# The normalisation of the expert results moved in among the expert tiles, with its transfers issued by ScalarE

## The reference

```python
x = x + _layernorm(_L0_attn_ref(_layernorm(x), wq, wk, wv, wo))
x = x + _layernorm(_L0_ffn_ref(_layernorm(x), g1, g2, w_down, ..., w1, w2, w3))
# the end of _L0_ffn_ref, with res the residual stream after its attention:
probs = jax.nn.softmax(t @ router_w, axis=-1)          # t: (4096, 128), 8 experts
vals, idx = jax.lax.top_k(probs, 2)
gate = ...                                             # two weights a token, sum 1
hid = silu(einsum('td,edf->tef', t, w1)) * einsum('td,edf->tef', t, w3)   # f: 256
y = einsum('ted,te->td', einsum('tef,efd->ted', hid, w2), gate)
return res + y
```

## Time and profile before

| | |
|---|---|
| runs | 777.09, 778.49, 778.08 us; median 778.08 |
| profiled execution | 779.29 us, its span 777.3 us |
| busy: TensorE, VectorE, ScalarE, GpSimd | 85%, 65%, 51%, 46% of the span |
| granted clock of TensorE, mean of the span | 0.950 of full |

### The profile page before, as it was taken

How to read it: one execution, slowest core, us unless ns; L and a number is a source line. 1 busy time by engine, 2 the same in 40 slices (tenths; PEclk the granted TensorE clock), 3 DMA queues, 4 the chain that set the end, 5 groups by cost and what they waited for, 6 DMA issues and landing times.

```text
span 777.3 us, 15273 instructions
## 1 busy us (share of the span) xinstructions
PE 660.4 (85%) x4861; PEld 394.9 (51%) x4914; DVE 503.1 (65%) x1623; ACT 396.0 (51%) x792; POOL 355.9 (46%) x398
## 2 busy tenths in 40 slices
PE   7976899999899799899989988979879799999900
PEld 3434456466466456546646644545534366666600
DVE  7465866968968677786876876766715144444456
ACT  3243376566476467456646635544521265655515
POOL 4150290391582566349147351640134155555565
PEclk9999799999999999999989999999989999999955
DMA  6101001001001000000100100100025332322163
GB/s 179 43 0 28 1 1 29 1 1 31 27 1 28 29 2 21 29 8 1 35 22 1 28 30 2 29 28 2 1 87 142 71 82 77 82 76 72 51 240 94
DMA packets 38008, 33.27 MB, mean 43 GB/s; under 512 B 6384, under 2 KB 33072, under 8 KB 37920
## 3 DMA queue, kind: packets, MB, share of 16 engines
q1 hardware_dynamic: 33616, 23.39, 11.3%
q0 software_dynamic: 4320, 8.92, 3.5%
HBM read 17.09 MB, written 12.01 MB: 37 GB/s over the span
## 4 chain that ended last, share of the span: by engine, by line
PE 51%; DVE 19%; POOL 14%; issue 9%; ACT 3%; SPq 2%; DMA 2%; another core or an unknown queue 1%; DVEq 0%; POOLq 0%; ACTq 0%
PE wide L979 8%; PE small L803 6%; PE small L758 5%; DVE nmax L1268 5%; PE wide L778 5%; PE small L995 4%; PE small L790 3%; PE small L820 3%; PE small L762 2%; PE small L849 2%; PE wide L733 2%; PE wide L783 2%; PE small L986 2%; POOL k_rows L1181 2%; DVE a_st L1249 2%
## 5 line engine op out<-in xcount | busy, mean ns | idle before, releaser
L1268 DVE TENSOR_REDUCE nmax<-small 128x1 f32<-128x512 f32 (+3 forms) x352 | 217.0, 637 | 66.2 <-PE small L762 46.9
L1077 ACT ACTIVATE pT<-wide 128x1024 f32<-128x1024 f32 x160 | 159.2, 1021 | 72.0 <-PE wide L783 57.5
L758 PE MATMUL small<-kz,qT 128*128 128x256 bf16 (+3 forms) x503 | 123.1, 306 | 22.1 <-DVE nmax L1268 15.4
L1197 POOL DMA_INDIRECT token_rows<-m_row,place_u x64 | 63.0, 984 | 122.3 <-DVE place_u L1473 85.7
L778 PE MATMUL wide<-qT,kz 128*128 128x384 bf16 (+3 forms) x492 | 95.4, 306 | 9.4 <-DVE qT L1414 7.6
L1215 POOL DMA_INDIRECT result_rows<-pT,dest x71 | 68.0, 957 | 67.8 <-issue 38.4
L803 PE MATMUL small<-pT,v_pad 128*5 128x512 f32 (+3 forms) x1024 | 82.0, 461 | 5.3 <-issue 5.3
L762 PE MATMUL small<-future_sb,idb 128*128 128x128 bf16 (+2 forms) x328 | 78.1, 238 | 0.6
L979 PE MATMUL wide<-kz,pT 128*128 x142 | 74.7, 608 | 1.4 <-ACT pT L1110 1.3
L758 PEld LDWEIGHTS small<-kz,qT 128*128 128x128 bf16 x512 | 43.9, 99 | 56.1 <-DVE nmax L1268 30.0
L1528 DVE TENSOR_TENSOR pT<-pT,wide 128x256 f32<-128x256 f32 x71 | 29.9, 421 | 61.2 <-ACT pT L1116 55.3
(11 more groups left out here) (200 smaller groups left out, 1248.4 us busy)
## 6 DMA issues: line engine op xcount, KB each, us to landing
pT<-token_rows SPq DMA_DIRECT2D x71, 65.0 KB
kz<-k_all SPq DMA_DIRECT2D x32, 128.0 KB, 2.4
kz<-result_rows SPq DMA_DIRECT2D x16, 256.0 KB, 5.5
x<-L_attn_x SPq DMA_DIRECT2D x8, 256.0 KB, 3.6
kz<-L_ffn_w SPq DMA_DIRECT2D x2, 1024.0 KB, 6.9
out<-x SPq DMA_DIRECT2D x8, 256.0 KB, 2.2
result_rows<-pT,dest POOLq DMA_INDIRECT x71
token_rows<-m_row,place_u POOLq DMA_INDIRECT x64
```

Source lines behind the costliest of these rows:

```text
L758: pe.matmul(bank[:, at:at + keys], qT1[:, m.parity, g, tile * P:(tile + 1) * P], kz[:, m.parity, g, r, 0:keys], start=(r == r0), stop=Fals ...
L1077: act.activation(pT[:, g % 2, s, :], wide[:, w % 2, :], ACT.Exp, scale=SCALE_B)\
L1197: pool.indirect_dma_start(token_rows[:, :], bass.IndirectOffsetOnAxis(ap=place_u[:, n, t:t + 1], axis=0), m_row[:, n, t, :], None).then_in ...
L1268: ins = dve.tensor_reduce(nmax[:, tile, g * R + r0:g * R + r0 + heads], bank[:, 0:heads * (tile + 1) * P].rearrange("p (h k) -> p h k", h= ...
```

## The change

**Order of the tiles.** The counts of every batch are kept (`totals`, from a fifth block of `f_rank`'s last matmul), and the tables are computed so that tiles are ordered by the batch of their first token. Before the tiles whose first token is in a batch after b there are then at most `8 (b + 1) + 7` tiles (`tiles_before_end_of`): 15, 23, ... 71. TensorE turns the two tables with two transposes so that SyncE and TensorE can read them (`tiles_read`, `read_u`).

**The end in pieces.** The end's work for batch b is called in the steps of the tiles, at fixed lags behind `tiles_before_end_of(b)`: loads at 4 to 7, pair 11, sum 13, statistics 14 and 15, mean 16, power 17, shift 19, norm 20 to 23, addition 25, stores 26 to 29. So the loads of batch 0 are in steps 19 to 22, those of batch 5 in 59 to 62. Batches 0 to 5 (`among_tiles`) load and store in pieces of 64 KB, eight loads and four stores each; batches 6 (loads at step 67) and 7 (step 75) in pieces of 256 KB. Steps from 72 on have no tile.

**Who issues.** ScalarE issues the loads of results and the stores, in its own order between `rows_turned` and `silu_of`; a batch's first load waits for all eight `y_out`. SyncE has only the loads of tiles left. `yin` now lies in four buffers that the tiles don't use.

```diff
+LOAD_AT, PAIR_AT, SUM_AT, MEAN_AT, POW_AT, SHIFT_AT, NORM_AT, OUT_AT, STORE_AT = 4, 11, 13, 16, 17, 19, 20, 25, 26
+
+
+def tiles_before_end_of(b):
+
+    return NE * (b + 1) + NE - 1
+
+
+def due(n, lag):
+
+    for b in range(NB):
+        if tiles_before_end_of(b) + lag == n:
+            return b
+    return None
+
+
+def among_tiles(b):
+
+    return tiles_before_end_of(b) + LOAD_AT + NT < TILES
+
+
+def last_steps(body):
+
+    for n in range(TILES + 1, tiles_before_end_of(NB - 1) + STORE_AT + 1):
+        body(n)
+
...
-        sel_before = sb("sel_before", [P, NT, NE], BF16)
+        sel_before = sb("sel_before", [P, NT + 1, NE], BF16)
+        totals = sb("totals", [P, NB + 1, NE])
+        row_of = sb("row_of", [P, 1])
...
-        yin = kz[:, :, :, :, :].rearrange("p a g r t -> p (a g r t)").bitcast(F32)\
-            .rearrange("p (b n t d) -> p b n t d", b=NB, n=TOP, t=NT)
-        pad_u, row_u, expert_u = (v.bitcast(U32) for v in (pad_uf, row_uf, expert_uf))
+            [[BUFS, ROW], [2, D], [2, F], [2, F], [2, F], [BUFS, D], [BUFS], [NE, NE], [NE], [NE],
+             [(NB + 1) * NE], [NB, NE], [NB * NE + 1], [NB, NE, NE], [NB * NE], [NB], [NB * NE + 1],
+             [2, NB * NE], [NB * NE], [2, NB * NE], [2], [1], [2], [2 * TILES]])
+
+        yin = [half.rearrange("p (n t d) -> p n t d", n=TOP, t=NT)
+               for flat in (a_p[:, :, :].rearrange("p t k -> p (t k)"), a_work[:, :, :].rearrange("p n w -> p (n w)"),
+                            q_rows[:, :, :, :, :, :].rearrange("p a t h s d -> p (a t h s d)").bitcast(F32),
...
 
             sp.wait_ge(small_free[last_ring.bank("f_pv3")], last_ring.count("f_pv3"))
-            for dst, src in ((full_sb, full_tiles), (numbers_sb, tile_numbers), (up_to_sb, up_to)):
...
             sp.wait_ge(spare_in, 16)
             sp.wait_ge(sent, 16 * TOP * NT * NB)
             tile_steps(lambda s: load_rows(s + 2), read_rows)
-
-            for i in range(BUFS):
-                sp.wait_ge(y_out[i], 16 * len(range(i, TILES, BUFS)))
-            for b in range(NB):
-                for n in range(TOP):
-                    at = n * NTOK + b * T
-                    sp.dma_start(yin[:, b, n, :, :], result_rows[at:at + T, :].rearrange("(p t) d -> p t d", t=NT))\
-                        .then_inc(yin_in[b], 16)
-            for b in range(NB):
-                sp.wait_ge(final_out, b + 1)
-                sp.dma_start(out[b].rearrange("(t p) d -> p t d", p=P), x1[:, b, :, :]).then_inc(out_done, 16)
-            sp.wait_ge(out_done, 16 * NB)
+            sp.wait_ge(out_done, 16 * sum(NT if among_tiles(b) else 1 for b in range(NB)))
 
...
+                        full(ring, step, pe.matmul(bank[:, 0:(NT + 1) * NE], ones[:, :],
                                                    sel_before[:, :, :].rearrange("p t e -> p (t e)"),
...
+                pe.wait_ge(small_free[bank], last_count[bank])
+            pe.wait_ge(tiles_placed, 1)
+            for n in range(2):
+                last = pe.transpose(small[0:1, 0, n * P:n * P + TILES], tile_at[0:TILES, n:n + 1], idf[0:TILES, 0:TILES])
+            last.then_inc(tiles_read, 1)
             pe.wait_ge(weights_in, 16 * N_WEIGHTS)
             pe.wait_ge(tables_done, 1)
...
+            def load_results(b, t):
+
+                if t == 0:
+                    for i in range(BUFS):
+                        act.wait_ge(y_out[i], 16 * len(range(i, tiles_before_end_of(b), BUFS)))
+                for n in range(TOP):
+                    at = n * NTOK + b * T
+                    rows = result_rows[at:at + T, :].rearrange("(p t) d -> p t d", t=NT)
+                    if among_tiles(b):
+                        act.dma_start(yin[b][:, n, t, :], rows[:, t, :]).then_inc(yin_in[b], 16)
+                    elif t == 0:
+                        act.dma_start(yin[b][:, n, :, :], rows).then_inc(yin_in[b], 16)
+
+            def store(b, t):
+                rows = out[b].rearrange("(t p) d -> p t d", p=P)
+                act.wait_ge(final_out, b + 1)
+                if among_tiles(b):
+                    act.dma_start(rows[:, t, :], x1[:, b, t, :]).then_inc(out_done, 16)
+                elif t == 0:
+                    act.dma_start(rows, x1[:, b, :, :]).then_inc(out_done, 16)
+
+            def normalise_results(b, t):
+                rstd, shift = ((a_rstd, a_nb), (p_rstd, p_m2))[b % 2]
+                if t == 0:
+                    act.wait_ge(final_shift, b + 1)
+                act.activation(yin[b][:, 1, t, :], yin[b][:, 0, t, :], ACT.Identity, bias=shift[:, t:t + 1],
+                               scale=rstd[:, t:t + 1]).then_inc(final_norm, 1)
+
+            def batch_step(n):
+                for t in range(NT):
+                    if due(n, LOAD_AT + t) is not None:
+                        load_results(due(n, LOAD_AT + t), t)
+                    if due(n, STORE_AT + t) is not None:
+                        store(due(n, STORE_AT + t), t)
+                    if due(n, NORM_AT + t) is not None:
+                        normalise_results(due(n, NORM_AT + t), t)
+
             def tile_step(s):
-                for part, tile in ((rows_turned, s + 2), (silu_of, s + 1), (hidden_turned, s)):
+                if (s + 2).exists():
+                    rows_turned(s + 2)
+                batch_step(s.n)
+                for part, tile in ((silu_of, s + 1), (hidden_turned, s)):
                     if tile.exists():
                         part(tile)
 
             tile_steps(tile_step)
-
-            for b in range(NB):
-                par = b % 2
-                rstd, shift = ((a_rstd, a_nb), (p_rstd, p_m2))[par]
-                act.wait_ge(final_shift, b + 1)
-                for t in range(NT):
-                    last = act.activation(yin[:, b, 1, t, :], yin[:, b, 0, t, :], ACT.Identity, bias=shift[:, t:t + 1],
-                                          scale=rstd[:, t:t + 1])
-                last.then_inc(final_norm, 1)
+            last_steps(batch_step)
 
         @block.gpsimd
         def _(pool):
...
-                pool.tensor_tensor(yin[:, b, 0, :, :], yin[:, b, 0, :, :],
-                                   yin[:, b, 1, :, :], ALU.add)\
+                pool.wait_ge(yin_in[b], 16 * TOP * (NT if among_tiles(b) else 1))
+                pool.tensor_tensor(yin[b][:, 0, :, :], yin[b][:, 0, :, :], yin[b][:, 1, :, :], ALU.add)\
                     .then_inc(pair_sum, 1)
 
-            add_pair(0)
-            for b in range(NB):
-                if b + 1 < NB:
-                    add_pair(b + 1)
+            def invert(b):
                 ve, rstd = ((a_ve, a_rstd), (p_ve, p_rstd))[b % 2]
                 pool.wait_ge(final_var, b + 1)
                 if b >= 2:
-                    pool.wait_ge(final_norm, b - 1)
+                    pool.wait_ge(final_norm, NT * (b - 1))
                 pool.tensor_tensor(rstd[:, :], ve[:, :], neg_half[:, :], ALU.pow).then_inc(final_pow, 1)
+
+            def batch_step(n):
+                if due(n, PAIR_AT) is not None:
+                    add_pair(due(n, PAIR_AT))
+                if due(n, POW_AT) is not None:
+                    invert(due(n, POW_AT))
+
+            def tile_step(s):
+                send_result(s + -1)
+                batch_step(s.n)
+
+            tile_steps(tile_step)
+            last_steps(batch_step)
 
         @block.vector
...
+                        dve.tensor_copy(totals[:, f.n, :], bank[:, NT * NE:(NT + 1) * NE])
...
+            table(dve.tensor_scalar(tiles_by[:, :], totals[:, :, :].rearrange("p b e -> p (b e)"), (P - 1) / 2, 1.0 / P,
+                                    ALU.add, ALU.mult))
+            table(dve.tensor_scalar(tiles_by[:, :], tiles_by[:, :], ROUND, None, ALU.add))
...
+            table(dve.tensor_tensor(parts_of[:, :, :], change[:, :, :],
+                                    at_end[:, :].unsqueeze(1).to_broadcast([P, 2, n_at]), ALU.mult))
+            table(dve.tensor_reduce(sums[:, :], parts_of[:, :, :], AX, ALU.add))
+            table(dve.tensor_scalar(tile_row[:, :], sums[:, 0:1], float(REGION // P), row_of[:, 0:1], ALU.mult, ALU.add))
+            table(dve.tensor_tensor(tile_row[:, :], tile_row[:, :], sums[:, 1:2], ALU.add))
+            table(dve.tensor_scalar(tile_at[:, 0:1], tile_row[:, :], float(P), None, ALU.mult))
+            dve.tensor_scalar(tile_at[:, 1:2], sums[:, 0:1], float(NE - 1), None, ALU.min).then_inc(tiles_placed, 1)
+            dve.wait_ge(tiles_read, 1)
+            dve.tensor_copy(read_u[0:1, :].rearrange("p (n c) -> p n c", n=2),
+                            small[0:1, 0, 0:2 * P].rearrange("p (n c) -> p n c", n=2)[:, :, 0:TILES]).then_inc(tables_done, 1)
...
+            def add_results(b):
+                dve.wait_ge(pair_sum, b + 1)
+                dve.tensor_tensor(yin[b][:, 0, :, :], yin[b][:, 0, :, :], res[:, b, :, :], ALU.add).then_inc(y_sum, 1)
+
+            def half_stats(b, half):
+                st = stats[b % 2][0]
+                if half == 0:
```

(40 more changed lines are left out.)

97 lines of the change are left out of this document (40 added, 57 removed).

## The result

| | median, us | runs | ratio to before, 95% interval |
|---|---|---|---|
| before | 778.17 | 4 | |
| after | 791.02 | 4 | 1.0165 (1.0132 to 1.0199) |

The forecast was 763.9, with a range of 758 to 771: the sign is wrong. The profiled spans are 777.3 and 789.4 us, 12.1 apart. The slices of the page of the kernel after are to be read against the earlier trace rows: of TensorE's two empty slices at the end one is left, but the tiles (the last slices but that one), which were six 9s in a row, now read 9, 7, 9, 9, 6, 8, 8.

What follows compares the result with a forecast made beforehand. TensorE bounds the tiles and idles in the end, where VectorE leads. End at 757.4 + 5.2 for ScalarE + 0.5 for counts = 763.1 us span, 765.1 profiled, less 1.2: forecast 763.9, range 758 to 771.

Steps and rivals of the forecast that it cites:

- the sign: Whole kernel: faster than before, chance 0.94; no change 0.02, slower 0.04.
- The end: After the last scatter: batch 7 alone remains, span ends at 757.4, which is 19.9 us less.
- SyncE and TensorE read the tables: Start of the tiles: SyncE reads the tables only at 609.55, after the padding; no price for TensorE's reads.
- Cover 5.5 us; nothing: Tables' chain before the tiles: ready at about 604, read by SyncE at 609.55, so it costs nothing.
- ScalarE's 5.2 us in the tiles: Issues and norm pieces on ScalarE delay the silu: 5.2 us at 0.35 per issue, 11.9 at 0.50.
- the case that issues are hidden: Rival for ScalarE in the tiles: issues done while it waits, period stays 1.64 us, time 758 to 761; chance 0.27.
- Every piece fits: VectorE in the tiles: pieces fit into its 0.84 us idle before the product and cost nothing.
- A late scatter is met only six steps later: GpSimd in the tiles: 3.0 us free in eight steps against 2.7 for pair and power, so nothing.
- not 2.8: VectorE's pieces in the tiles: without cover 2.8 us per batch, some 17 us for six.

Runs made afterwards that it cites:

- e1: The kernel after with the experts' table starting at element 72 instead of 71, a multiple of 16 bytes: 776.81 us, ratio 0.9991 to before.
- e2: The kernel before with its experts' table moved by three elements, to 12 bytes past a multiple of 16: 793.23 us, ratio 1.0190.
- e13: e1 with pieces later, ScalarE copying the turned tables, 20 keeping-warm matmuls behind the transposes and 8 instead of 26 behind the read: 766.18 us, ratio 0.9891.
- e15: e13 without loads of results and stores among the tiles (batches 0 to 6): 769.90 us in one run, before beside it 775.39.
- e4: e1 with loads of results and stores issued by SyncE, five steps later, instead of ScalarE: 773.44 us, ratio 0.9942 to before.
- e5: e1 with the steps of a batch's end moved later (sum 15, power 19, shift 22, stores from 29): 779.00 us, ratio 1.0053 to before.
- e10: e4 with the pieces later still (shift 25, stores from 32) and ScalarE copying the turned tables: 773.48 us, ratio 0.9945 to before.
- e14: e13 with SyncE issuing the loads of results and the stores instead of ScalarE: 763.02 us, ratio 0.9864 to before.
- e12: e4 with 20 keeping-warm matmuls behind the transposes and 8 instead of 26 behind the read: 739.85 us, ratio 0.9914; before there 746.78.
- e11: e1 with pieces later, ScalarE copying the turned tables, no result loads or stores among the tiles; on a chip where before takes 746.78 us.
- the four pairs: Kernels differing by issuer alone; SyncE's median lower by 3.4 us (e1, e4), 7.1 (e5 and its SyncE version), 1.9 (e10 and its ScalarE version), 3.2 (e13, e14).

## Why the prediction was wrong

**The end: right.** 17.1 us from the last scatter on were forecast and 18.1 measured.

**"SyncE and TensorE read the tables": the step that is missing.** The forecast priced the tables' chain and found it covered ("Cover 5.5 us; nothing"), but said nothing of what TensorE's reads cost. The diff moves the experts' table from a place of its own, which `carve` begins at a multiple of four elements, to element 71 behind the other table, and that word position makes each read 4.0 us dearer. e1 and e2 give it 13 to 15 us, the clock it costs included. It makes the change slower; without it (e1) the change is level with before, and still not the 14 us faster that were forecast. The read of before (1671/1825/2145 ns) was in the trace; I had looked at SyncE's row of the same line in the chain and not at TensorE's, and no row of before could have shown what a start off a multiple of 16 bytes does.

**"about 604. Cover 5.5 us; nothing": the cover was SyncE's, not TensorE's.** The chain's length was right. The copy then came some 4.5 us behind the transposes, for which I had given the hand-over next to nothing, and TensorE has 26 matmuls to do between its read and the first tile, so it has no cover. With the alignment mended the start is still 3.8 us late; e13 to e15, which put 20 matmuls into the wait and leave 8 behind the read, take back all of it.

**ScalarE's 5.2 us in the tiles: the size may stand, the way it was summed doesn't.** The issues have the forecast size, but e4 (none on ScalarE) loses the same 13.3 us in the tiles as e1, so the ordinary issue of 0.33 to 0.46 us doesn't add up step by step. What the traces show instead is a single long one (2.53 us in e5) in front of a silu. The medians of the four pairs put ScalarE's issues at 1.9 to 7.1 us, which takes in the 5.2. By the Trainium skill, "Perfetto Trace Analysis", section "DVE / Act Engine Instruction", which the prediction weighed for the case that issues are hidden, an instruction that waits in its engine's queue leaves the sequencer free for the next one. The trace of e5 agrees: the activation in front of the long issue ran beside it, at 699.71, and the silu behind it waited.

**"Every piece fits" and "A late scatter is met only six steps later": the step that failed in the tiles.** It summed free time over eight steps and looked at late scatters only. It left out that VectorE's own queue stands at the sum until GpSimd's pair is done, and at the shift until the power is: 9 us of such waits in e1 and 16 in e4. But with these waits taken away (e10, e14) the loss stayed at 12 to 14 us, now where TensorE's counts come late. On the one chip without late counts the tiles lose 10.0 us with GpSimd's waits and SyncE's transfers (e12) and 1.5 without either (e11). Since e14 and e13 against e15 price the transfers at 0.7 to 1.8 on another chip, GpSimd's lateness is the likely owner of the rest there, which is argued and not shown. One sum of this part is off too: by its rows the work on VectorE is 3.0 us a batch and not 2.8; nothing hangs on it.

**Open.** Why TensorE's counts come late on all chips but one, why more often in some versions of the program than in others, and whether its matmuls themselves are late or their counts alone (the profile models the ends of matmuls). For the transposes it isn't the shape, nor the counting instruction, nor TensorE's idleness, nor the reading engine. Open too are the length of the longest issues and the 2.8 us ahead of the first scatter.

## What to carry to other kernels

When a table that an engine reads into registers changes its place in a buffer, look at its first byte: here 12 bytes off cost 13 to 15 us in three reads, and all the added issues together 2 to 7. Free time of an engine summed over eight steps says nothing about an engine queued behind it: for each added wait ask how many steps lie between the producer's start and the consumer's place. Idle time without a named releaser isn't idle time without a cause: look for its length among the ordinary waits, and for the time of the count that it waited for. And an experiment that lands on another chip is only evidence beside a kernel traced there.

## Not expected of the hardware

- A register read of 24 words by TensorE took 1.6 to 2.3 us from a start at a multiple of 16 bytes and 5.6 to 6.1 us from 12 bytes past one (two kernels against all the others). SyncE's reads were always from multiples of 16 bytes and say nothing.
- A semaphore counted by TensorE behind two small transposes released VectorE, and ScalarE alike, 4.5 to 4.7 us after they began, in thirteen kernels, in four of them while 20 matmuls went through in the meantime. In the two kernels on the chip of e11 and e12 it was 0.33 us.
- In the tiles TensorE's counts usually stand 0.29 us behind the issue. On the same chips several at a time came up to 4.5 us late within 0.2 us of each other, at places that stayed with the program; on the chip of e11 and e12 none did.
- One issue of a 64 KB store by ScalarE took 2.53 us where its like took 0.38, and the silu behind it waited for it.
- One chip ran the kernel before in 746.8 us where the others took 775 to 779.
